# A planned Mamba and soft-MoE kernel: TensorE's products laid out anew, skip tiles moved apart, and one tile of every state given to ScalarE

## What is computed

```
x = x + layernorm(attn(layernorm(x)))       # attn: two Mamba blocks in a row, plus their input
x = x + layernorm(soft_moe(layernorm(x)))

def mamba_block(x):                          # x 8192 x 512, inner width 1024, 16 states
    xc, z = split(x @ W_in.T)
    u     = silu(causal_conv4(xc) + b_c)
    dt, B, C = split(u @ W_x.T)              # 32, 16, 16 columns
    delta = softplus(dt @ W_dt.T + b_dt)
    h_t   = exp(delta_t * A) * h_(t-1) + delta_t * u_t * B_t     # for 1024 x 16 states
    y     = (sum over states of C_t * h_t + u * D) * silu(z)
    return y @ W_out.T
```

## Time and profile before

| | |
|---|---|
| median of 3 runs | 8613.96 us (8612.18 to 8619.41) |
| profiled execution | 8617.45 us, of which its span 8615.6 us |
| busy: PE, DVE, ACT, POOL | 86%, 88%, 68%, 76% of the span |

### The profile page before, as it was taken

One profiled execution on the slowest core, in us unless ns is written; L12 is line 12 of the kernel. 1 busy time (PEld: TensorE's weight loads), 2 busy tenths in 40 slices (PEclk: granted clock), 3 DMA queues, 4 the chain that ended last, 5 costly groups with the idle time before them and its releaser, 6 DMA issues. The chain is left out here.

```text
span 8615.6 us, 126403 instructions
## 1 busy us (share of the span) xinstructions
PE 7396.0 (86%) x31688; PEld 4113.0 (48%) x31688; DVE 7620.8 (88%) x8802; ACT 5873.9 (68%) x10702; POOL 6574.0 (76%) x2826
## 2 busy tenths in 40 slices
PE   5788888888888888888888888888888888876886
PEld 3444444444444444444444444444444444445753
DVE  2899999999999999999999999999999999995717
ACT  5777777777777777777777767777777777754415
POOL 0888888888888888888888888888888888881103
PEclk7899999999999999999999999999999999977889
DMA  5111111111111111121111111111111111114434
GB/s 197 49 51 50 46 50 51 51 51 52 53 51 47 51 52 49 45 63 61 61 51 52 51 52 46 51 51 48 46 50 51 51 52 50 47 37 153 166 127 148
DMA packets 223573, 552.99 MB, mean 64 GB/s; under 512 B 26272, under 2 KB 26528, under 8 KB 201824
## 3 DMA queue, kind: packets, MB, share of 16 engines
q1 hardware_dynamic: 196448, 459.30, 17.0%
q10 hardware_dynamic: 26368, 84.95, 2.5%
HBM read 442.44 MB, written 101.71 MB: 63 GB/s over the span
## 5 line engine op out<-in xcount | busy, mean ns | idle before, releaser
L931 POOL TENSOR_TENSOR bu<-w,b_rep 128x1024 f32<-128x1024 f32 x2048 | 4808.6, 2361 | 956.0 <-DVE h L1007 955.9
L1007 DVE TENSOR_TENSOR_SCAN h<-decay,h_last,bu 128x512 f32<-128x512 f32 x3840 | 4817.3, 1271 | 200.1 <-PE turn L519 140.6
L728 ACT ACTIVATE decay<-delta,neg_a 128x512 f32<-128x512 f32 x4096 | 2802.7, 689 | 1862.4 <-DVE h L1007 1848.1
L519 PEld LDWEIGHTS turn<-ident_m,h 128*128 128x128 f32 x16384 | 1918.4, 143 | 3163.2 <-DVE acc L1027 1246.1
L519 PE MATMUL turn<-ident_m,h 128*128 128x128 f32 x16384 | 2591.6, 282 | 615.3 <-DVE acc L1027 359.3
L1027 DVE SCALAR_TENSOR_TENSOR acc<-turn,c_now,acc 128x512 f32<-128x512 f32 x3200 | 2327.5, 727 | 191.9 <-PE turn L519 185.8
L448 PE MATMUL proj<-conv_in,conv_diag 128*128 128x512 f32 x2048 | 1039.7, 596 | 45.7 <-ACT halo L662 45.7
L448 PE MATMUL proj<-x_conv,w_in 128*128 128x512 f32 x2048 | 1055.5, 613 | 22.0 <-DMA x_conv<-xt 17.0
L448 PE MATMUL proj<-x_gate,w_in 128*128 128x512 f32 x2048 | 1034.2, 597 | 43.1 <-ACT stage L718 29.5
L448 PE MATMUL proj<-zy,w_out 128*128 128x512 f32 x2048 | 1033.7, 599 | 0.9 <-DVE zy L1036 0.9
L946 POOL TENSOR_TENSOR acc_v<-acc_v,prod 128x1024 f32<-128x1024 f32 x320 | 755.2, 2360 | 16.7 <-ACT prod L742 16.7
(11 more groups left out here) (171 smaller groups left out, 5947.0 us busy)
## 6 DMA issues: line engine op xcount, KB each, us to landing
b_rep<-b_rows SPq DMA_DIRECT2D x1024, 256.0 KB, 3.3
x_conv<-xt SPq DMA_DIRECT2D x32, 1024.0 KB, 6.5
x_gate<-xt SPq DMA_DIRECT2D x32, 1024.0 KB, 4.8
xt<-stage ACTq DMA_DIRECT2D x128, 256.0 KB, 2.4
x_n<-in_x_dram SPq DMA_DIRECT2D x16, 1024.0 KB, 5.2
xt<-xt_n ACTq DMA_DIRECT2D x16, 1024.0 KB, 4.3
x_l<-in_x_dram SPq DMA_DIRECT2D x16, 1024.0 KB, 5.8
mt_l<-xt SPq DMA_DIRECT2D x16, 1024.0 KB, 6.3
```

The costliest lines, as they stand in the source:

```text
L519: mm = pe.transpose(out[:, b * P:(b + 1) * P], h[:, k % 2, b, j * P:(j + 1) * P], ident[:])
L728: act.activation(decay[:, b, :], delta[:, blk, :], ACT.Exp, scale=neg_a[:, n, blk:blk + 1]).then_inc(decay_set, 1)
L931: pool.tensor_tensor(bu[:, s // 2 % 4, :, :], w[:, blk:blk + 2, :], b_rep[:, k % 4, :].unsqueeze(1).to_broadcast([P, 2, T]), ALU.mult).the ...
L1007: dve.tensor_tensor_scan(h[:, k % 2, b, :], decay[:, b, :], bu[:, s // 2 % 4, b % 2, :], start, ALU.mult, ALU.add).then_inc(scanned, 1)
```

## The change

1. **Products by time.** `timetable` no longer counts 1.17 products per slot. Each slot has a share of TensorE's time, and what its tiles weigh comes off; a product goes into a slot while at least half of its weight is left. Weights are in units of one product: 0.55 a state tile, 1.05 a skip tile.
2. **Skip tiles apart.** They stood in slots 0 to 3 and 32 to 35. Now they stand in slots 4 to 7, and in 30, 33, 36 and 39. The four y tiles of the second half move from slots 20, 22, 24, 26 to 22, 24, 26, 28.
3. **Every state gives one tile to ScalarE.** Before, 28 of the 32 groups did; states 4 and 5 of each half (`q % 8 == 2`) did not. `prod` gets four buffers for two, and the sums of a pair stand two `inputs` later (`SUM_LAG_Q`).
4. **One x buffer.** `x_conv` and `x_gate` become one buffer that is loaded twice per chunk, at group 1 for the next chunk's input projection and at group 18 for the gates.

The tables that come of it move ScalarE's fetches too. `silu_u` of the first half was at position 37 and is at 44; that of the second half was at 61 and is at 72; `silu_z` of the second half was at position 0 of the next chunk and is at 1. `delta` 4 and 5 with their `exp` and `ln`, which were at 7, 11, 12 and 13, are at 4, 5, 6 and 7. The first `sum_next` of GpSimd was at slot 98 and is at 106, the second was at 110 and is at 114.

```diff
-ORDER = [("conv_half", 0, 0), ("delta", 4, 0), ("conv_half", 1, 0), ("delta", 5, 0), ("conv", 0, 0), ("conv_half", 2, 0),
+ORDER = [("delta", 4, 0), ("delta", 5, 0), ("conv_half", 0, 5), ("conv_half", 1, 0), ("delta", 6, 0), ("conv", 0, 0),
...
-RATE = 1.17
...
+Y_AT = ((116, 118, 120, 122), (22, 24, 26, 28))
+SKIP_AT = ((7, 4, 5, 6), (30, 33, 36, 39))
...
+WEIGHT = {"x_proj": 1.1, "delta": 1.25, "delta_next": 1.25, "turn_c": 0.5, "state": 0.55, "skip": 1.05, "y": 0.55}
...
 def timetable():
-    at, end_of = 0.0, {}
+    room = [-sum(WEIGHT[tile[0]] for tile in tiles_at) for tiles_at in TURN_AT]
+    whole = sum(PRODUCTS[kind] * WEIGHT.get(kind, 1.0) for kind, _, _ in ORDER) - sum(room)
+    room = [r + whole / (SLOTS_BODY - 3) for r in room]
+    slot, left, end_of = 0, room[0], {}
...
-        slots = [int(at + q / RATE) for q in range(PRODUCTS[kind])]
-        at += PRODUCTS[kind] / RATE
...
+        slots = []
+        for q in range(PRODUCTS[kind]):
+            while left < WEIGHT.get(kind, 1.0) / 2 or slot < earliest:
+                slot += 1
+                left = min(left, 1.0) + room[slot]
+            slots.append(slot)
+            left -= WEIGHT.get(kind, 1.0)
...
-Y1_AT = (20, 22, 24, 26)
-SKIP_AT = (0, 8)
...
 V_AT = (0, 3)
+V_SETS = 4
...
-    return tile[0] == "skip" or tile[0] == "state" and tile[1] // 2 in V_PAIRS and tile[2] == V_AT[tile[1] % 2]
+    return tile[0] == "skip" or tile[0] == "state" and tile[2] == V_AT[tile[1] % 2]
...
-        mine = [(4 * q + 11, ("pair", q))] if q % HALF_Q else []
+        mine = [(4 * q + SUM_LAG_Q, ("pair", q))] if q % HALF_Q else []
         if q % HALF_Q == HALF_Q - 1:
-            mine.append((4 * q + 13, ("join", q // HALF_Q)))
+            mine.append((4 * q + SUM_LAG_Q + 1, ("join", q // HALF_Q)))
...
-    x_conv = sb("x_conv", [P, KD, T])
-    x_gate = sb("x_gate", [P, KD, T])
+    x = sb("x_m", [P, KD, T])
...
-    prod = sb("prod", [P, 2, 2, HB * P])
+    prod = sb("prod", [P, V_SETS, 2, HB * P])
...
+        def load_conv(G, layer, kind):
+
+            last_half = 2 * NB - 2 if kind.first else proj_base(G, kind)
+            sp.wait_ge(proj_full, last_half)
+            load_x(G + 1, layer)
+
+        def load_gate(G, kind):
+
+            halves = 0 if kind.last else kind.place[ORDER.index(("conv_half", NB - 1, 0))] + 1
+            sp.wait_ge(proj_full, proj_base(G, kind) + halves)
+            load_x(G, kind.layer)
```

More of the change, by code:

```diff
@@ L35 @@
 RING = 2
-ORDER = [("conv_half", 0, 0), ("delta", 4, 0), ("conv_half", 1, 0), ("delta", 5, 0), ("conv", 0, 0), ("conv_half", 2, 0),
[L41 to L45, removed]
+ORDER = [("delta", 4, 0), ("delta", 5, 0), ("conv_half", 0, 5), ("conv_half", 1, 0), ("delta", 6, 0), ("conv", 0, 0),
+         ("conv_half", 2, 0), ("delta", 7, 0), ("conv", 1, 0), ("conv_half", 3, 0), ("conv", 2, 0), ("conv_half", 4, 0),
+         ("conv", 3, 0), ("conv_half", 5, 0), ("conv", 4, 0), ("conv_half", 6, 0), ("conv", 5, 0), ("conv_half", 7, 0),
+         ("conv", 6, 0), ("out", 0, 0), ("conv", 7, 0), ("out", 1, 0), ("x_proj", 0, 0), ("turn_c", 0, 0), ("out", 2, 0),
+         ("delta_next", 0, 0), ("out", 3, 0), ("delta_next", 1, 0), ("gate", 0, 0), ("delta_next", 2, 0), ("gate", 1, 0),
+         ("delta_next", 3, 0)] + [("gate", b, 0) for b in range(2, NB)]
 PRODUCTS = {"delta": 1, "conv_half": KD, "conv": TAPS, "out": NB, "x_proj": NB, "delta_next": 1, "turn_c": 1, "gate": KD}
@@ L405, in body @@
                     load_skip_weights(new)
-                if k == 25 and next_but_one < LAYERS and not kind.last:
-                    load_conv(G + 2, next_but_one)
+                if k == 18:
+                    load_gate(G, kind)
                 if k == 27 and before_last and new < LAYERS:
@@ L555, in _ @@
             for half in (b, b + 1):
[L556 removed]
+                conv_half(prologue_bank(n), 1, 0, half, (0, KD))
                 n += 1
@@ L593, in body @@
                     if what == "gate":
-                        gate(out, G, kind.layer, x, (lo, hi))
+                        gate(out, 2 * G + (3 - kind.last), kind.layer, x, (lo, hi))
         all_chunks(pe, body)
@@ L737, in product @@
                 act.wait_ge(c_set, 2 * G + (k // HALF_C + 1))
-            of_last, reader = reader_before(q)
-            if k % 2 == 0 and not (kind.first and of_last):
-                act.wait_ge(vsum_set, sum_base(G, kind) + (kind.sums.index(reader) + 1 + C_PROD))
-            act.activation(prod[:, V_SET[q], k % 2, :], turn[:, BANK[tile], :], ACT.Copy,
+            if k % 2 == 0 and not (kind.first and q < V_SETS):
+                reader = reader_before(q)
+                at = kind.sums.index(reader) if q >= V_SETS or reader in SUMS_CARRIED else SUMS.index(reader) - len(SUMS)
+                act.wait_ge(vsum_set, sum_base(G, kind) + (at + 1 + C_PROD))
+            act.activation(prod[:, q % V_SETS, k % 2, :], turn[:, BANK[tile], :], ACT.Copy,
                            scale=c_now[:, j, n:n + 1]).then_inc(v_done, 1)
@@ L821, in take_tiles @@
                 if what == "conv":
-                    conv(src, G + 1, turn_base(*now) + (now[1].turns.index["skip", x // HB, J - 1] + 1), x)
+                    conv(src, G + 1, turn_base(*now) + (now[1].turns.index[LAST_SKIP[x // HB]] + 1), x)
                 if what == "silu_u":
```

104 lines of the change are left out of this document (47 added, 57 removed).

## The result

The changed kernel takes 8636.5 us (median of 9 runs) against 8615.2 for the one before: ratio 1.0025, interval 1.0015 to 1.0035. It is slower by 0.25%, where 8470 was forecast. The profiled execution has a span of 8634.7 us and a mean granted clock of 0.949.

The account below looks back on a forecast made before the run. VectorE's own list plus its waits was taken to bound each chunk. Loss of 14.1 us before, less 12.2 after, plus 2.6 for additions gave 4.5 per chunk, times 32 = 144 us: 8470 us, 8-in-10 range 8375 to 8565.

Parts of the forecast that it names:

- One x buffer. Same bytes ... 0.: Load of x for slot 5, issued at slot 125: costs 0, up to 1 us if GpSimd waits for B rows.
- The 0.6 for scan 0: Jump to the loop's head: TensorE's and ScalarE's delays stay as they were, costing 0.6 us per chunk.
- Doubles just before a slot 4k cost 0.5: Two products in the slot before a slot 4k (88 and 104) cost 0.5 us in all, from 0 to 2.
- "0.9" for slots 32 to 40: Skips at 30, 33, 36, 39: scan 40 is 0.7 us late and slot 32 gets 0.2, 0.9 in all.
- "1.9" for the SiLU: SiLU of u moved to 44 and 72: tiles 46 and 48 and the decay of scan 73 late, 1.9 us.
- 4.2: Skip tiles in slots 4 to 7: ScalarE's list delays the addition of slot 6, then scan 8; 4.2 us lost.
- I take 0.8: Skip tiles meeting TensorE's slow clock, partly hidden by ScalarE's waits: 0.8 us, from 0 to 3.
- scan 116 ... 2.8 lost: Slots 106 to 116: GpSimd's twelve operations, 27.8 us, make scan 116 wait; 2.8 us lost per chunk.
- without that cover it would cost up to 1: GpSimd's crowd at slots 10 to 22: late bu of slot 22 covered by the skips' loss, otherwise up to 1 us.
- Four additions less ... 2.6: Slots 16 to 31 and 80 to 95: four fewer VectorE additions at 0.65 us each take off 2.6 us per chunk.
- the slow clock holds through the skips: Rival: TensorE at 1.2 GHz in slots 4 to 9 and perhaps 36 to 42, 4.7 us per chunk slower, 8764; chance 0.08.
- Dense layout: Rival: TensorE at 90% in all slots passes ScalarE's delays to tile 4k; 4.2 us lost, 8604 us; chance 0.08.

Follow-up runs that it names:

- e_load_held: Changed kernel with SyncE's load of the next x put behind B row 4 and held until scan 0 of the new chunk is done; 8605.9 us, ratio 0.9991.
- e_timetable_load: As e_timetable, but the load of the next chunk's x is put where the changed kernel has it, ahead of B row 1; 8677.4 us, ratio 1.0076.
- e_comb_fill: Changed kernel with e_load_held, e_take_early, SiLU and skips moved, SUM_LAG_Q 11, first second-layer tile transposed four times, state tiles of slots 1 to 4 twice; 8391.8 us.
- e_comb_fill_load: e_comb_fill with the load of x back in the jump, where the changed kernel has it; 8375.3 us, ratio 0.9720.
- e_comb_fill3: e_comb_fill with the state tiles of slots 1 to 4 transposed three times instead of twice; 8356.6 us, ratio 0.9700.
- e_take_early: Changed kernel with ScalarE's fetch of conv_half 1 and gate 0 from their PSUM banks one position earlier; 8596.5 us, ratio 0.9979.
- e_exp_later: Changed kernel with exp and ln of delta 4 and 5 four positions later and GpSimd's sum and product of them two later; 8636.8 us, ratio 1.0029.
- e_best: e_comb_fill3 with exp and ln of delta 4 and 5 four positions later, as in e_exp_later; 8357.1 us, ratio 0.9700.
- e_timetable: Kernel before the change with only the new order of products, skip tiles and y tiles; x buffers, additions, prod buffers and sums as before; 8633.7 us, ratio 1.0027.

## Why the prediction was wrong

*"One x buffer. Same bytes ... 0."* The first step that failed. It asked whether x comes in time for slot 5 and whether B rows come late, not what else uses the DMA engines: the engines' own code, fetched at the same jump. The 0.6 for scan 0 was "taken unchanged" and measured 3.3, and slots 1 to 3 lost 1.5 for 0.5, all of it in the second layer, where TensorE stops once more behind its first tile: 5.0 us with the load beside it, 2.5 without (e_load_held). That is 3.7 of the 6.0 us between 12.2 and 18.2. What the load costs in the end depends on its surroundings: 44 us in e_timetable_load, 30 in the changed kernel (e_load_held), and from e_comb_fill to e_comb_fill_load it even gained 16. Against e_comb_fill3, which has the full clock without the load, e_comb_fill_load is 19 us slower, with fewer repeated tiles.

*The list of waits had no bank of the `proj` ring.* Fetching two banks one position earlier takes 1.46 us off slot 15 and 0.89 off slot 103 (e_take_early), 2.35 us per chunk that no term of the sum stood for. The forecast followed the ring of turn banks tile by tile and never did the same for the products.

*"Doubles just before a slot 4k cost 0.5", "0.9" for slots 32 to 40, "1.9" for the SiLU* were right in kind: 0.7 (slots 87 and 103 without the ring's share), 1.9 and 2.5.

*The skips: "4.2", and "I take 0.8" for the clock.* The sum of 5.0 measured 4.0, a size that came near by luck, for the split was wrong. ScalarE's list, the reason given for the 4.2, was not what ended the waits: moving `exp` and `ln` away did nothing for the time (e_exp_later), because the stall at the jump had let ScalarE catch up, and in the first layer TensorE's slow clock stood in front. Where both are gone the list is there at its price, 4.3 us (e_comb_fill3), of which e_best takes 1.5 away.

*GpSimd: "scan 116 ... 2.8 lost".* Right. The twelve operations took 28.05 us for 27.8; the loss was 1.9 because the ring had made VectorE 0.9 late at slot 103, and 2.8 where it had not (e_take_early). The warning for slot 22, "without that cover it would cost up to 1": no run waited there, but with `ln` four positions later such a wait came at scans 16 and 18, 1.1 us (e_best).

*"Four additions less ... 2.6".* Right: eight slots with six additions take 13.35 us. As a whole: the new order alone was to gain 4.7 us per chunk and lost 0.7 (22 us in all, e_timetable), the load cost 44, and the rest of the change (four additions less, GpSimd's crowd, the later sums) gave 41.

The rival "the slow clock holds through the skips" asked for 10 us of low level past slot 4; it had 5.3 in the first layer and 1.5 in the second, and was the closest of the three in mechanism. "Dense layout" came nearest in time (8604), but its condition did not come: the clean groups of eight still take 13.35 us. What stays open: which part of the low clock in slots 4 to 8 of e_comb_fill comes from where in the chunk's start, and whether moving `ln` by two positions instead of four would keep both gains of e_best; neither was run.

## What to carry to other kernels

Ask of each moved transfer what else needs the DMA engines at that moment, and count the code fetch after a loop's jump among it. Follow every ring of buffers, not only the one next to the bound: a one-product tile in a ring of two makes its neighbour wait. And price a removed stall by what it had been covering; here the stall at the jump hid ScalarE's list, and ScalarE's list hid GpSimd's crowd. Four edits worth 30 to 80 us each gave 230 us together, more than their sum, and keeping up TensorE's clock gave 50 more.
